# Two layer-norm applies on ScalarE instead of VectorE, half of one stage's PSUM copies on VectorE, and mask loads in another order

## What is computed

```python
# block mask: a 32x32 block of the weight counts if any mask entry in it is set
bm = mask.reshape(Nb, 32, Kb, 32).sum(axis=(1, 3)) > 0
w  = (weight.reshape(Nb, 32, Kb, 32) * bm[:, None, :, None]).reshape(N, K)
x  = x + layernorm( layernorm(x) @ w.T + bias )
h  = layernorm(x)
top1  = argmax(h @ gate_w.T + expert_bias)          # 4 experts, lora rank 8
x  = x + layernorm( h @ W_up.T + lora(h, top1) )
```

## Time and profile before

| | us |
|---|---|
| median of 2 timed runs | 1737.62 (1736.26 to 1738.98) |
| profiled execution | 1662.72 |
| its span, slowest core (core 7) | 1661.2 |
| spans of the 8 cores | 1648.5 to 1661.2 |
| mean granted TensorE clock of the cores | 0.883 to 0.889 |
| busy in the span: PE, PEld, DVE, ACT, POOL | 1108.2, 869.3, 601.1, 355.6, 78.9 |

### The profile page before, as it was taken

One profiled execution on the slowest core, in us unless ns is written; L12 is line 12 of the kernel. 1 busy time (PEld: TensorE's weight loads), 2 busy tenths in 40 slices (PEclk: granted clock), 3 DMA queues, 4 the chain that ended last, 5 costly groups with the idle time before them and its releaser, 6 DMA issues.

```text
span 1661.2 us, 26697 instructions; the slowest of 8 cores (1648.5 to 1661.2 us)
## 1 busy us (share of the span) xinstructions
PE 1108.2 (67%) x9240; PEld 869.3 (52%) x9240; DVE 601.1 (36%) x861; ACT 355.6 (21%) x1185; POOL 78.9 (5%) x96
## 2 busy tenths in 40 slices
PE   0211269888999998989311312799999999999700
PEld 0100147667777776777200101577777777777600
DVE  1566664555555565453544354100000000000571
ACT  1111212122222222222323322222222222222200
POOL 1000000000000000000000000000000000000141
PEclk9999999999999999999655555799999999999955
DMA  8923226676687767661423373124324423432379
GB/s 195 319 76 101 42 60 146 160 190 165 163 200 185 188 180 179 170 138 55 152 102 152 127 192 142 47 53 79 74 52 77 77 52 58 84 64 52 105 278 376
DMA packets 40000, 220.47 MB, mean 133 GB/s; under 512 B 4850, under 2 KB 4866, under 8 KB 21442
## 3 DMA queue, kind: packets, MB, share of 16 engines
q0 software_dynamic: 11792, 84.46, 25.9%
q1 hardware_dynamic: 23330, 100.74, 18.0%
q10 hardware_dynamic: 4752, 33.56, 5.3%
HBM read 252.86 MB, written 33.55 MB: 172 GB/s over the span
## 4 chain that ended last, share of the span: by engine, by line
PE 49%; DVE 20%; DMA 17%; issue 8%; ACT 3%; DVEq 1%; ACTq 0%; POOLq 0%; POOL 0%; SPq 0%
PE pm L382 41%; DMA mring<-mw 13%; DVE psj_i L310 4%; PE pt L219 3%; DVE wmb L353 3%; DVE sums_h L262 2%; PE pm L219 2%; ACT junk L532 2%; PE pm L396 2%; DVE xbst L277 1%; DMA mo<-x 1%; DVE mo L546 1%; DMA y<-wmb 1%; DVEq L691 1%; DVE cmp L572 1%
## 5 line engine op out<-in xcount | busy, mean ns | idle before, releaser
L382 PE MATMUL pm<-wmb,fm 128*128 128x256 bf16 x8192 | 952.7, 275 | 38.9 <-DVE zfm L596 0.7
L382 PEld LDWEIGHTS pm<-wmb,fm 128*128 128x128 bf16 x8192 | 791.4, 99 | 177.6 <-issue 80.7
L402 ACT ACTIVATE mo<-pm 128x256 bf16<-128x256 f32 x256 | 98.3, 384 | 795.8 <-PE pm L389 418.8
L310 DVE TENSOR_REDUCE psj_i<-mring 128x32 int32<-128x1024 int32 x128 | 156.1, 1220 | 216.3 <-DMA mring<-mw 209.6
L188 DVE TENSOR_REDUCE st_d<-acc_s 128x1 f32<-128x16 f32 x8 | 1.4, 170 | 489.8 <-ACT junk L410 489.1
L219 PE MATMUL pt<-identb,xbst 128*128 128x128 bf16 x264 | 40.8, 288 | 193.3 <-DVE xbst L277 183.8
L353 DVE TENSOR_TENSOR wmb<-wmb,bmpj 128x4096 bf16<-128x4096 bf16 x32 | 141.6, 4425 | 13.2 <-DMA wmb<-bw 10.1
L219 PEld LDWEIGHTS pt<-identb,xbst 128*128 128x128 bf16 x264 | 22.7, 115 | 211.4 <-issue 205.3
L410 ACT ACTIVATE junk<-pm 128x256 bf16<-128x256 f32 x256 | 98.3, 384 | 23.5
L219 PE MATMUL pm<-identb,mo 128*128 128x128 bf16 x152 | 27.4, 288 | 47.4 <-DVE mo L546 41.9
L342 POOL DMA_DIRECT2D wmb<-bu x32 | 17.4, 544 | 749.5 <-PE pm L396 414.6
(11 more groups left out here) (128 smaller groups left out, 446.0 us busy)
## 6 DMA issues: line engine op xcount, KB each, us to landing
mring<-mw SPq DMA_DIRECT2D x128, 512.0 KB, 5.2
wmb<-bw POOLq DMA_DIRECT2D x32, 1024.0 KB, 9.6
wmb<-bu POOLq DMA_DIRECT2D x32, 1024.0 KB, 8.0
mo<-x POOLq DMA_DIRECT2D x12, 1024.0 KB, 24.0
xst<-x SPq DMA_DIRECT2D x10, 1024.0 KB, 7.1
xmid<-xst ACTq DMA_DIRECT2D x10, 1024.0 KB, 3.9
fm<-xmid SPq DMA_DIRECT2D x8, 1024.0 KB, 9.9
y<-fm ACTq DMA_DIRECT2D x8, 1024.0 KB, 17.6
```

The costliest lines, as they stand in the source:

```text
L310: return e.tensor_reduce(out=psj_i32[:, (j % 2) * 256 + pc * 32:(j % 2) * 256 + (pc + 1) * 32], in_=mring[idx % 2][:, :].rearrange("p (g w ...
L382: return e.matmul(bank[0:128, 0:NS], fm[:, k * 1024 + i * 128:k * 1024 + i * 128 + 128], wmb[j % 2][:, k * NS:(k + 1) * NS], start=(k == 0 ...
L402: return e.activation(out=mo[:, i * 4096 + j * NS:i * 4096 + (j + 1) * NS], in_=bank[0:128, 0:NS], func=AF.Identity, accum_out=acc_s[:, i ...
```

## The change

Four edits. (1) The apply of stage 2 runs on ScalarE, as an Identity activation with a per-partition scale and bias, instead of VectorE's tensor_scalar. (2) The same for the apply of stage 4. (3) In stage 4 the copies of the even transpose groups stay on ScalarE and those of the odd groups go to VectorE; the gate matmuls and the writers of `mo` wait for the last two copies instead of the last. (4) In stage 2, the first four pieces of mask 0 come behind chunk 0 and the other four behind chunk 1; mask 1 (pieces, convert, matmul, compare) comes behind chunk 7 instead of behind chunks 3 and 5.

```diff
@@ transpose_chunk
-                t_ev = E(evac_eng, fe, waits=[t_tr],
-                         inc="sA" if evac_eng == "scalar" else "sV")
+                ee = evac_eng if evac_eng != "alt" else ("scalar" if g % 2 == 0 else "vector")
+                t_ev = E(ee, fe, waits=[t_tr],
+                         inc="sA" if ee == "scalar" else "sV")
@@ rec_p2_chunk
-                    return e.tensor_scalar(
+                    return e.activation(
                         out=xbst[:, h * HALF:(h + 1) * HALF],
-                        in0=ap_slot,
-                        scalar1=rqP2[:, pr * 2:pr * 2 + 1],
-                        scalar2=rqP2[:, pr * 2 + 1:pr * 2 + 2],
-                        op0=ALU.mult, op1=ALU.add)
-                ap = E("vector", fa, waits=[t_r, t_qq, half_toks[h][1],
-                                            (tr_done.get(c - 1) or [None])[-1]], inc="sV")
+                        in_=ap_slot, func=AF.Identity,
+                        scale=rqP2[:, pr * 2:pr * 2 + 1],
+                        bias=rqP2[:, pr * 2 + 1:pr * 2 + 2])
+                ap = E("scalar", fa, waits=[t_r, t_qq, half_toks[h][1],
+                                            (tr_done.get(c - 1) or [None])[-1]], inc="sA")
@@ order of stage 2
         rec_p2_chunk(0)
+        rec_mask_pieces(0, range(0, 4))
         rec_p2_chunk(1)
-        rec_mask_pieces(0); rec_mask_cvt(0)
+        rec_mask_pieces(0, range(4, 8)); rec_mask_cvt(0)
         rec_p2_chunk(2)
         rec_mask_gbm(0)
         rec_mask_tt_half(0, 0); rec_mask_tt_half(0, 1)
         rec_p2_chunk(3)
-        rec_mask_pieces(1); rec_mask_cvt(1)
         rec_p2_chunk(4)
         rec_p2_chunk(5)
-        rec_mask_gbm(1)
         rec_p2_chunk(6)
         rec_p2_chunk(7)
+        rec_mask_pieces(1); rec_mask_cvt(1)
+        rec_mask_gbm(1)
@@ stage 4
-                ap = E("vector", lambda e, ...: e.tensor_scalar(
+                ap = E("scalar", lambda e, ...: e.activation(
...
             tr_done[("p4", i)] = transpose_chunk(
-                i, ap, src=xb4, slots_l=pt + pm_tr,
+                i, ap, src=xb4, slots_l=pt + pm_tr, evac_eng="alt",
                 extra_w=[ev_tok[JN * TC - 1], tr_done[TC - 1][-1]])
-            zw = [tr_done[("p4", i)][-1], t_ag, z_tok.get(i - 2),
-                  bm_tok.get(JN - 2 + (i % 2))]
+            zw = [tr_done[("p4", i)][-1], tr_done[("p4", i)][-2], t_ag,
+                  z_tok.get(i - 2), bm_tok.get(JN - 2 + (i % 2))]
```

More of the change, by code:

```diff
@@ L545, in build_program @@
             for h in range(2):
[L546 to L550, removed]
+                ap = E("scalar", lambda e, h=h, pr=pr, xb4=xb4, ap_slot=slots[h][0]: e.activation(
+                    out=xb4[:, h * HALF:(h + 1) * HALF], in_=ap_slot,
+                    func=AF.Identity,
+                    scale=rqP4[:, pr * 2:pr * 2 + 1],
+                    bias=rqP4[:, pr * 2 + 1:pr * 2 + 2]),
                     waits=[t_r3, t_q3, hts[h][1],
-                           r1_tok.get(i - 1)], inc="sV")
+                           r1_tok.get(i - 1)], inc="sA")
             apply4_tok[i] = ap
             tr_done[("p4", i)] = transpose_chunk(
-                i, ap, src=xb4, slots_l=pt + pm_tr,
+                i, ap, src=xb4, slots_l=pt + pm_tr, evac_eng="alt",
                 extra_w=[ev_tok[JN * TC - 1], tr_done[TC - 1][-1]])
-            zw = [tr_done[("p4", i)][-1], t_ag, z_tok.get(i - 2),
-                  bm_tok.get(JN - 2 + (i % 2))]
+            zw = [tr_done[("p4", i)][-1], tr_done[("p4", i)][-2], t_ag,
+                  z_tok.get(i - 2), bm_tok.get(JN - 2 + (i % 2))]
             mmz = None
@@ L618, in build_program @@
                         (tr_done.get(("p4", i + 1)) or [None])[-1],
+                        (tr_done.get(("p4", i + 1)) or [None, None])[-2],
                         apply4_tok.get(i + 1)]
```

## The result

| | before | changed |
|---|---|---|
| median of the timed runs, us | 1661.57 (8 runs) | 1693.68 (9 runs) |
| ratio changed to before | | 1.0187, 95% interval 1.0169 to 1.0204 |
| span of the profiled execution, us | 1661.2 | 1686.5 |
| busy PE, DVE, ACT, us | 1108.2, 601.1, 355.6 | 1112.4, 572.6, 404.1 |

The change makes the kernel 1.9% slower (1.7 to 2.0%), about 31 us. The forecast was +18.8 us and 1756.4 us, with a range of 1741 to 1772. So the absolute number missed its range, and the change came out larger than its forecast by some 12 us.

A forecast was written before the change was run, and what follows sets the result against it. The prediction took stages 2 and 4 as bound by one chain walking from engine to engine, no engine full. Stage 2's +9.0 and stage 4's +9.8 gave +18.8 us on 1737.6: 1756.4 us, range 1741 to 1772.

The forecast's parts named there:

- the 74.9 us that were carried over: Whole kernel: timed median 1737.6 us lay 74.9 above the profiled execution's 1662.7; the unplaced difference was kept in the forecast.
- The sum: Stage 2 +9.0 us and stage 4 +9.8, stages 3, 5 and 6 unchanged: +18.8 us.
- so nothing is won or lost there: Apply to transposes: the hand-over from ScalarE to PE takes 0.24 us, so it adds nothing.
- the term of the mask's split: Stage 2, mask 0 in two portions of four pieces: 23.1 us instead of 26.15, so 3.0 less.
- Both rivals on stage 3: Stage 3 falls into step with the mask (1734 us, chance 0.11) or further out of step (1770 to 1784, 0.09).
- the one in which the apply hides: Stages 2 and 4: ScalarE's apply runs beside VectorE's work, 48.8 us leave the path, 1685 us; chance 0.03.
- The apply's term: Stages 2 and 4: both halves take 4.45 us instead of 3.05, 1.40 more a chunk, 11.2 us per stage.
- the bound that the prediction gave it: Mask 0's split in stage 2: slower landing of pieces could cost 5 us more, making it a loss of 2.
- The exposed matmul of mask 1: End of stage 2: mask 1's matmul ahead of column 0 waits for copy and convert; together +0.8 us.
- its two terms: Stage 4: the apply on ScalarE +11.2 us, the odd copies on VectorE -1.4 us.
- a stage 3 out of step: Stage 3: mask later by one or two us in each of 14 columns, 14 or 28 us more; chance 0.09.

The follow-up runs named there:

- e5: The kernel before with only the apply of stage 4 moved to ScalarE, copies unchanged; ratio 1.0054, 1670.7 us.
- e2: The kernel before with only one more wait, on a ScalarE semaphore reached long before, on the transposes of stage 2; ratio 1.0040, 1670.6 us.
- e3: The changed kernel, with TensorE leaving out every wait its own list has already asked for; ratio 1.0056 against the kernel before, 1672.8 us.
- e7: The kernel before, with TensorE leaving out every wait its own list has already asked for; ratio 0.9913, 1650.4 us.
- e1: The kernel before with only the apply of stage 2 moved to ScalarE; ratio 1.0081, 1676.4 us.
- e4: The kernel before with only the new order of the mask pieces; ratio 1.0015, 1664.6 us.

## Why the prediction was right and where it failed

Three steps failed. The absolute number failed by its base, the 74.9 us that were carried over; the runs put the kernel before at 1661. The sum failed in stage 2 by the step "so nothing is won or lost there" (a wait more in every group, some 7.6 us) and by the term of the mask's split, -3.0, which was +1.0.

- **The mechanism was right.** A chain through several engines, in which the load of an engine does not count; the apply on ScalarE without cover; stage 3's own work untouched (557.3 and 557.5 us on the middle core). A chunk of stage 4 follows the other after 31.97 us (32.0 forecast). PE's waits for converts in stage 3 are 25.5 us in 8 places (29.4 in 9 before), apart from the 22.0 us that the matmul of mask 1 waits ahead of column 0. Both rivals on stage 3 fell, and so did the one in which the apply hides.
- **The apply's term was right.** L278 takes 2.093 us on average against the 2.10 taken, and e5 shows 11.2 us for eight chunks. The square beside it still takes 1.910. If function and accumulator make no difference, which no run isolates, two per-partition operands cost 0.183 us. The Trainium skill (ScalarE: Activation LUTs, section "What ACT_TABLE_LOAD costs") states some 93 ns for each such operand, and the trace agrees. The rule of the Trainium skill to keep add and mul on VectorE (same page, section "Rules for kernel authors") holds here as well: no edit that moved a whole apply gained anything.
- **The term that was missing.** "From ScalarE to PE takes 0.24 us, so nothing is won or lost there" looked at the hand-over and not at what the transposes then wait for. With the apply on ScalarE the fourth transpose of each group asks for a fourth semaphore: 64 x 0.106 = 6.8 us in stage 2. The first transpose of a chunk asks for one more too and starts 0.35 instead of 0.25 us behind the apply, 0.8 us in eight chunks. e2 shows the wait in isolation, e3 takes it away. The trace of before held the answer: 0.75 us a group in stage 2 with three waits at the fourth transpose and 0.86 in stage 4 with four. The prediction put the second number down to PE at its low clock, and e3 and e7 show that it was the waits.
- **The mask's term had the wrong sign.** -3.0 for the split became +1.0: the first four pieces took 17.9 us instead of 14.1 and the others 9.2 instead of 9.0. The 14.1 was read where the transfers of x were about to end (DMA share 0.94 from 75 to 80 us and 0.13 from 80 to 83 before, 1.00 from 54 to 72 in the changed kernel), and the piece that came late now (70.47) had come with its neighbour then (82.23). The miss of 4 us lies within the bound that the prediction gave it (5 us more, a loss of 2). The exposed matmul of mask 1 is there: convert at 252.36, its matmul at 253.01, column 0 at 253.54.
- **What was overlooked about cover.** The mask wait of before hid lateness: in e1 and e2 the first two chunks' extra time vanished in it. In stage 2 the changed kernel is e4 with the first edit, and there this edit costs 251.5 - 234.3 = 17.2 us; in the old order (e1) it cost 12.5. So in the new order the hidden 4 us come back: chunk 0 ends its copies 1.9 us later than in e4, and chunk 1 starts its own 3.2 us later, the 1.9 and the apply's 1.4 in full (medians of the cores).
- **The sum.** Stage 2, apply 11.2, one more wait and later start 6.8 + 0.8, mask +1.0 and +0.8: 20.6, where the middle core shows 18.8 and the two profiled slowest cores 20.0 (253.54 - 233.52). The 2 us between them are not placed. Stage 4: 9.9 measured, 9.8 forecast, and its two terms hold by themselves (e5 11.2, and 1.3 for the copies beside it).
- **The base.** The forecast carried 74.9 us over from two timed runs ("whose extra time no row here places"), although the profiled execution spoke for 1662.7. On that base the same sum gives 1681.5, still 12 us short, and mostly by the missing term. The range would have become 1666 to 1697 and held the 1693.7, but by luck in part: its upper end was put there for a stage 3 out of step, which did not come.

## What to carry to other kernels

In a chain that walks from engine to engine, moving a link to the idler engine costs the difference of their speeds unless something else runs in its place; split the link so that the next one can start on the first half. Count the waits that every short instruction issues before and after, fulfilled ones too: an edit that changes who produces an operand can add one. Work fed by a ring belongs in portions of the ring's size between pieces of other work; larger portions bring the transfer's latency back.

## What the runs showed of the hardware that was not expected

- A wait on a semaphore that has long had its value is not free on TensorE's queue. A group of four 128 x 128 transposes takes 0.73 us when the fourth asks for nothing, 0.75 when it asks for three semaphores, and 0.86 when it asks for four. The fourth costs 0.106 us, the first three together 0.02. The packed traces show why the steps differ. The fourth transpose starts 0.27, 0.34 and 0.44 us behind the first (e3, before, changed), so three waits do delay it by 0.07. But it then takes 0.27 us instead of the 0.31 that it takes right behind its neighbours, by the profile's modelled ends. And the next group starts 0.15 us behind its end in all three kernels, since its first transpose waits for it.
- These 0.73 and 0.86 us are the same at a granted clock of 1.00 (stage 2, 2.4 GHz) and of 0.50 (stage 4, 1.2 GHz): the granted clock doesn't set the pace there. The waits do, the one for the group before and those of the fourth transpose.
- Stage 3 was left as it was by waits skipped, orders changed and 55 us of earlier start: its median over the cores lies between 554.6 and 560.3 us in all 14 kernels, and the cores of one execution lie further apart than that.
